# Two eight-batch attention blocks around a latent-attention block: reciprocal norms broadcast inside SBUF, and a new task order in the feed-forward phases

## The chip, the core and the metric

The kernel runs on one core of a Trainium2 chip. A core has five engines with an instruction queue each: TensorE (PE, matrix products), VectorE (DVE), ScalarE (ACT), GpSimd (POOL) and SyncE (SP). In this kernel SP computes nothing: it issues every DMA. Engines wait for one another through semaphores, and each works through its own list strictly in order. The metric is the time on the device in microseconds, the median of several executions.

## The reference

The input x is [8, 512, 128] in fp32. It passes through three residual blocks:

```python
x = x + 0.5 * ffn(layernorm(x), ...)      # phase 1, two layers
x = x + attn(layernorm(x), ...)           # the latent-attention block
x = x + 0.5 * ffn(layernorm(x), ...)      # phase 3, the same two layers again
```

What is called ffn holds two layers, and each layer is a local attention followed by a gated feed-forward part:

```python
h = shift_token(x)                         # half of the channels come from the token before
q, k, v = split(h @ wqkv)                  # 8 heads of 64
q = l2norm(q) * qs;  k = l2norm(k) * ksc   # l2norm(t) = t / ||t||, per token and head
q, k = rotary_xpos(q, k)
o = local_attention(q, k, v)               # windows of 64, own window and the one before, softmax
x = x + o @ wo
h = layernorm(shift_token(x)) * lg + lb
a, g = split(h @ w1 + b1)                  # HID = 341
x = x + (a * gelu(g)) @ w2 + b2
```

The part that the change touches is l2norm: a sum of squares over the 64 channels of each head, the power -1/2 of it, and a multiplication of q and k with it.

## The kernel before

**The layout.** Channels or heads lie on partitions, the 512 tokens of a batch element (T) on the free axis. A feed-forward phase (`ffn_phase`, run twice) handles 16 units: unit u is layer u // 8 of batch element u % 8. A unit passes through some thirty tasks. Each engine has a loop over n and runs in each iteration a list of tasks for the units n+1, n, n-1, ..., n-4, so up to five units are in flight (a software pipeline). The list, `run(task, n - k, ...)`, is a table written out by hand for each engine; that order and the semaphores decide everything, and no scheduler is at work. One iteration in the steady state is called a cycle below, and it advances every unit by one place. Eight PSUM banks are handed from task to task with `claim`, which makes PE wait until the last reader of a bank is done.

**q and k.** `project(u, m)` for m = 0..3 multiplies with wqkv in a split precision (three matmuls for each half) into banks 4 and 5. (m even: q, m odd: k; the pair 0, 1 serves heads 0 to 3, the pair 2, 3 heads 4 to 7.) ACT squares the two banks into `SQ[:, m, 0]` and `SQ[:, m, 1]` (`square_a`, `square_b`). DVE multiplies each bank with the rotary tables into `TP` (`rotate(u, m, 1)` and `rotate(u, m, 0)`, L782), and POOL combines these into `QK[:, m]` (`rotate`, L936 and L937). There is one `TP`: DVE may fill it for m+1 only after POOL has read it for m (`ad_ok`).

**The norms.** After the fourth square PE sums them over the heads (`norms`, L467; below "the norm sums") into a bank in which partition 8j holds one of sixteen rows (m, i): pair m, head i of the group. DVE clamps (`clamp`, L788), ACT forms exp(-0.5 ln) (L657, L658), and DVE makes one Newton step (`norms`, L793 to L796). Now RN holds 16 reciprocal norms, in rows of 512 tokens. They have to stand on all 32 partitions of their head before POOL can multiply `QK` with them. SP does this with a trip through DRAM: it stores `RN[0:P:8]` to `norms_d` (L363), waits for it to land (`r_out`), waits until POOL no longer needs the old values (`nr_ok`), and loads them back with four broadcasting DMAs, each into 32 partitions of `SQ[:, :, 1]` (L369). POOL waits for all four (`r_in`) and multiplies `QK[:, m]` with `SQ[:, m, 1]` (`norms`, L942). The first group of scores needs m = 0 and 1, the second m = 2 and 3.

**Attention.** `scores(u, g)` (L475 the mask, L484 the products) fills banks 0 to 3 for heads 4g to 4g+3. DVE takes the maxima (L805), PE transposes them (`turn_max`), DVE spreads them (`spread_max`, L812 and L816), PE adds them to the scores (`add_max`, L498), ACT exponentiates (`softmax_exp`). PE sums (`sums`, L506), ACT inverts the sums, SP sends them through DRAM (`sums_d`, L380 and L386) into `OT`. PE multiplies with v (`attend`, L517), DVE multiplies by the inverse sums (`attended`, L823), and PE applies wo (`join`, L527).

**The gated part.** `center`, `variance`, `hidden` (six thirds, L552), `gate`, `gated` (L848) and `outward` (L560) follow, with the variances sent through DRAM as well (`vars_d`, L391). `statistics` and `tokens` on DVE, `tokens` (L435) on PE bring in the next batch element (layer 0 only); `back` takes it out. `values` (L456) makes v, `high` and `low` (L633, L928) split the next unit's input into two parts, on which the next `project` waits.

**The queue of SP** runs in each iteration values, variances, sums for group 0, sums for group 1, norms.

**The latent-attention block** (`mla_phase`) lies between the two phases and takes its folded weights `Wq_s`, `Wk_s`, `Wv_s` from tiles that the setup wrote and that stay in SBUF during phase 1.

## Time and profile before

| | us |
|---|---|
| median of 3 runs | 2268.1 (2256.44 to 2269.57) |
| the profiled execution, its time | 2281.34 |
| the profiled execution, its span | 2279.2 |

| busy share of the span | PE | PE weight loads | DVE | ACT | POOL |
|---|---|---|---|---|---|
| whole kernel | 81% | 49% | 63% | 49% | 40% |

The setup ends at about 43 us, the first feed-forward phase at 917 us, the latent-attention block between 918 and about 1440 us, and the second feed-forward phase fills the rest. The granted clock of TensorE is 0.915 in the mean.

How to read it: a row of the timeline gives the start, the duration, the engine, the line and the operation, `x4` for four that follow one another, and in square brackets the idle time of the engine ahead of it with what ended it. `SPq` is the issue of a DMA by SP. A matmul of 512 fp32 columns counts as two instructions there. A row of the waits gives the engine that waited, for whom, the sum in us, how many times, and the longest. A row of the windows gives for a stretch the busy time of each engine, PE's granted clock (1.00 is 2.4 GHz, 0.50 is 1.2 GHz), the busy share of the DMA engines and the GB/s that they moved.

### The profile page before, as it was taken

To read this page: it belongs to the slowest core of one execution; us is meant where nothing else is said; L and a number is where in the kernel's file an instruction comes from. 1 tells how busy PE (TensorE), PEld (TensorE's weight loads), DVE (VectorE), ACT (ScalarE), POOL (GpSimd) and SP (SyncE) were. 2 spreads that over 40 slices of the span, in tenths; PEclk is the share of its full clock that TensorE was granted. 3 is DMA by queue.
4 is the path that set the end of the run, shared out by engine and by line. 5 is a ranking of instruction groups with operands and counts; after the bars stand their busy time and mean duration, and the time that the engine had idled before them with its cause. 6 is when DMAs were issued, how large, how long until landed. Compare 5 with 4: busy or idle time off the path is not lost. (4 is left out here: it accounts for less than half of the span.)

```text
span 2279.2 us, 50236 instructions
## 1 busy us (share of the span) xinstructions
PE 1837.4 (81%) x20010; PEld 1120.2 (49%) x20074; DVE 1444.4 (63%) x2281; ACT 1117.9 (49%) x2070; POOL 901.3 (40%) x624
## 2 busy tenths in 40 slices
PE   1577888888888787799999996677788888887886
PEld 1344454544555454466666663344454544544543
DVE  2466766566665644688888885566666665555563
ACT  1134444354444433488888884234434444444342
POOL 2444444454444440222222222444544444444440
PEclk9888999899999989799999997789989898999899
DMA  3122223222222321000000000123322222233221
GB/s 123 36 59 61 69 70 93 62 60 66 68 68 73 84 60 29 1 2 1 2 1 2 1 1 1 46 60 87 76 60 60 61 73 60 70 90 77 64 65 42
DMA packets 60664, 118.84 MB, mean 52 GB/s; under 512 B 7519, under 2 KB 17939, under 8 KB 58259
## 3 DMA queue, kind: packets, MB, share of 16 engines
q1 hardware_dynamic: 60435, 115.64, 20.0%
q8 instruction: 162, 2.65, 0.5%
q14 instruction: 67, 0.55, 0.1%
HBM read 82.51 MB, written 3.74 MB: 38 GB/s over the span
## 5 line engine op out<-in xcount | busy, mean ns | idle before, releaser
L942 POOL TENSOR_TENSOR QK<-QK,SQ 128x1024 f32<-128x1024 f32 x128 | 298.3, 2352 | 190.6 <-DMA SQ<-norms_d 190.6
L782 DVE SCALAR_TENSOR_TENSOR TP<-bank,cols,tab 128x1024 f32<-128x1024 f32 x256 | 320.4, 1275 | 47.2 <-PE bank L447 34.5
L805 DVE TRANSPOSE_TENSOR_REDUCE MX<-bank 128x16 f32<-128x512 f32 x256 | 160.4, 684 | 264.6 <-PE bank L484 264.6
L936 POOL TENSOR_TENSOR QK<-TP 128x512 f32<-128x512 f32 x128 | 164.3, 1283 | 407.8 <-DVE TP L782 260.4
L1195 ACT ACTIVATE PL<-bank,NM 128x384 f32<-128x384 f32 (+3 forms) x512 | 255.5, 540 | 15.6 <-DVE NM L1275 12.7
L1275 DVE TENSOR_REDUCE NM<-bank 128x1 f32<-128x384 f32 (+3 forms) x352 | 217.7, 635 | 35.4 <-PE bank L1109 31.7
L475 PE MATMUL bank<-bandb,identb 128*128 128x512 bf16 x192 | 74.5, 510 | 180.8 <-POOL QK L942 178.0
L1118 PE MATMUL bank<-cst,PL 128*128 128x128 f32 x1280 | 200.0, 275 | 3.3 <-DVE PTL L1284 1.1
L639 ACT ACTIVATE SQ<-bank 128x512 f32<-128x512 f32 x128 | 76.5, 598 | 239.7 <-PE bank L447 239.7
L1104 PE MATMUL bank<-KL,QZL 128*128 128x384 f32 (+3 forms) x512 | 189.3, 422 | 2.3 <-DVE QZL L1232 2.3
L484 PEld LDWEIGHTS bank<-QK 32*64 32x64 f32 x8192 | 155.8, 162 | 40.8 <-issue 40.8
L484 PE MATMUL bank<-QK 32*64 32x128 f32 x8192 | 170.1, 322 | 0.3 <-issue 0.3
L1187 ACT ACTIVATE PTL<-bank 128x512 f32<-128x512 f32 (+1 forms) x288 | 161.5, 561 | 13.0 <-PE bank L1118 9.8
L517 PEld LDWEIGHTS bank<-PT,V 128*64 128x64 f32 x4096 | 132.6, 142 | 68.4 <-issue 49.1
L937 POOL TENSOR_TENSOR QK<-TP 128x512 f32<-128x512 f32 x128 | 165.6, 1294 | 0.0
L447 PE MATMUL bank<-HTH,wqkv_h 128*128 128x512 f32 x256 | 136.9, 535 | 25.2 <-DVE TP L782 17.6
L645 ACT ACTIVATE SQ<-bank 128x512 f32<-128x512 f32 x128 | 76.5, 597 | 160.0 <-DVE TP L782 96.3
L1315 POOL TENSOR_SCALAR QZL<-QS,cst 128x512 fp32r<-128x512 f32 x64 | 108.2, 1701 | 116.3 <-DVE QS L1222 116.2
L682 ACT ACTIVATE DC<-bank 128x512 f32<-128x512 f32 x32 | 19.2, 599 | 267.8 <-PE bank L534 267.8
L651 ACT ACTIVATE V<-bank 128x512 f32<-128x512 f32 x128 | 76.5, 598 | 148.2 <-PE bank L456 141.9
L823 DVE TENSOR_TENSOR OT<-bank,OT 128x512 f32<-128x512 f32 x128 | 82.2, 684 | 104.1 <-DMA OT<-sums_d 104.0
L517 PE MATMUL bank<-PT,V 128*64 128x64 f32 x4096 | 145.8, 229 | 0.9 <-DVE OT L823 0.8
(171 smaller groups left out, 3777.1 us busy)
## 6 DMA issues: line engine op xcount, KB each, us to landing
SQ<-norms_d SPq DMA_DIRECT2D x128, 256.0 KB, 4.9
OT<-sums_d SPq DMA_DIRECT2D x128, 256.0 KB, 3.9
V<-V SPq DMA_DIRECT2D x32, 512.0 KB, 7.7
V<-V SPq DMA_DIRECT2D x32, 384.0 KB, 8.8
RB<-vars_d SPq DMA_DIRECT2D x32, 256.0 KB, 3.2
X<-in_L_attn_x SPq DMA_DIRECT2D x8, 256.0 KB, 4.4
out<-X SPq DMA_DIRECT2D x8, 256.0 KB, 8.5
wqkv_raw<-in_L_ffn_wqkv SPq DMA_DIRECT2D x1, 1536.0 KB
```

Source lines behind the costliest of these rows:

```text
L484: last = nc.tensor.matmul(BK[i][e * W:(e + 1) * W, k0:k0 + n], QK[r, 2 * g + 1, z, k0:k0 + W], QK[r, 2 * g, z, k0:k0 + n], start=False, st ...
L517: last = nc.tensor.matmul(BK[k][e * W:(e + 1) * W, w * W:(w + 1) * W], (V1, V0)[w % 2][:, w // 2, h * DH:(h + 1) * DH], PT[:, j // 2, h % ...
L782: nc.vector.scalar_tensor_tensor(out=TP[:, o:o + 2, :], in0=BK[4 + z][:, :].unsqueeze(1).to_broadcast([P, 2, T]), scalar=q, in1=tab[:, e, ...
L805: last = nc.vector.tensor_reduce(MX[:, i, :], BK[i][:, :].rearrange("p (a b) -> p a b", b=32), AX_X, ALU.max, apply_transpose=True)
L936: nc.gpsimd.tensor_tensor(QK[:, m, 0, :], TP[:, 2, :], TP[:, 1, :], ALU.subtract)
L937: nc.gpsimd.tensor_tensor(QK[:, m, 1, :], TP[:, 0, :], TP[:, 3, :], ALU.add).then_inc(S["ad_ok"], 1)
L942: nc.gpsimd.tensor_tensor(QK[:, m, :, :], QK[:, m, :, :], SQ[:, m, 1, :].unsqueeze(1).to_broadcast([P, 2, T]), ALU.mult).then_inc(S["nr_ok ...
L1104: nc.tensor.matmul(bank[:, h * N:(h + 1) * N], QZL[:, G % 2, h0 + h, i * P:(i + 1) * P].bitcast(F32R), KL[:, G % 2, 0:N].bitcast(F32R), st ...
L1118: last = pe.transpose(BK[B_PT[k % 2]][:, j * P:(j + 1) * P], PL[:, k % PRING, j * P:(j + 1) * P], ident)
L1187: nc.scalar.activation(dst, src, ACT.Copy).then_inc(S["pta_ok"], 1)
L1195: last = nc.scalar.activation(PL[:, m % PRING, h * N:(h + 1) * N], BK[m % SRING][:, h * N:(h + 1) * N], ACT.Exp, bias=NM[:, m % SRING, h:h ...
L1275: nc.vector.tensor_reduce(NM[:, m % SRING, 0:n], BK[m % SRING][:, 0:n * N].rearrange("p (h k) -> p h k", h=n), AX_X, ALU.max, negate=True) ...
```

## The change

Four things are changed.

1. The norms no longer go through DRAM. `norms` on SP issues sixteen DMAs from SBUF to SBUF, each of which reads one row of RN (one partition, 2 KB) 32 times and writes it to 32 partitions of a tensor of its own, `RB` (64 KB each, 1 MB for a unit, as before). They are issued m by m, and each m has its semaphore, so that POOL can multiply m = 0 when four of the sixteen have landed.
2. `SQ[:, m, 1]` is no longer written by DMA. ACT's `square_b` waits for the norm sums of the unit before (`ss_in`), and no more for POOL's multiplication.
3. RB takes 8 KB of each partition. U and `stats` shrink, and the folded weights are stored to DRAM during the setup (`folded_d`) and loaded back at the start of the latent-attention block.
4. The order of the tasks in the loops of all five engines is another.

```diff
                         def norms(u):
                             sp.wait_ge(S["nw_ok"], u + 1)
-                            sp.dma_start(norms_d[u % 2], RN[0:P:8, :]).then_inc(S["r_out"], 16)
-                            sp.wait_ge(S["r_out"], 16 * (u + 1))
                             if u >= 1:
                                 sp.wait_ge(S["nr_ok"], 4 * u)
-                            for i in range(4):
-                                src = norms_d[u % 2].rearrange("(c i) n -> i c n", i=4)[i]
-                                sp.dma_start(SQ[32 * i:32 * i + 32, :, 1, :],
-                                             src.unsqueeze(0).broadcast_to([32, 4, T])).then_inc(S["r_in"], 16)
+                            for m in range(4):
+                                for i in range(4):
+                                    src = RN[32 * m + 8 * i:32 * m + 8 * i + 1, :]
+                                    sp.dma_start(RB[32 * i:32 * i + 32, m, :], src.unsqueeze(1).broadcast_to([1, 32, T])).then_inc(S[f"r_in{m}"], 16)
...
                         def square_b(u, m):
                             act.wait_ge(S["nb_ok"], 4 * u + m + 1)
                             if u >= 1:
-                                act.wait_ge(S["nr_ok"], 4 * (u - 1) + m + 1)
+                                act.wait_ge(S["ss_in"], u)
...
                         def norms(u, m):
                             pool.wait_ge(S["ad_ok"], 4 * u + m + 1)
-                            pool.wait_ge(S["r_in"], 64 * (u + 1))
+                            pool.wait_ge(S[f"r_in{m}"], 64 * (u + 1))
...
+                    sp.wait_ge(copied, 8)
+                    sp.dma_start(folded_d, fold[:, :]).then_inc(kept, 16)
+                    sp.wait_ge(kept, 16)
...
                     def _(sp):
+                        sp.dma_start(fold[:, :], folded_d).then_inc(S["fold_in"], 16)
                         for last_use in used:
                             sp.sem_clear(last_use)
...
                         xt(0)
+                        pe.wait_ge(S["fold_in"], 16)
                         values(0)
```

The order on **SP** in the steady state, from one unit's inverse sums to the next variances. Before, with the trip through DRAM:

```order
L380 DMA sums_d<-DR 4x512
L386 DMA OT<-sums_d 64x2x512 x2
L363 DMA norms_d<-RN 16x512
L369 DMA SQ<-norms_d 32x4x512 x4
L374 DMA V_1<-V_1 64x2048
L375 DMA V_1<-V_1 64x1536
L391 DMA vars_d<-RV 4x128
```

And in the changed kernel (its lines are three higher from here on):

```order
L383 DMA sums_d<-DR 4x512
L389 DMA OT<-sums_d 64x2x512 x2
L373 DMA RB<-RN 32x1x512 x16
L377 DMA V_1<-V_1 64x2048
L378 DMA V_1<-V_1 64x1536
L394 DMA vars_d<-RV 4x128
```

The place of the norms in the queue has stayed, behind the second sums and ahead of the copy of v; one store and four loads have become sixteen copies.

On **PE** around the norm sums (`bank<-SQ,cst`). Before, the outward product (`bank<-GL,w_s`) stands behind the norm sums, and one of four attend groups (x16 each) ahead of them:

```order
L498 MATMUL bank<-CB,pick 128x512 x4
L517 MATMUL bank<-PT,V_1 64x64 x16
L467 MATMUL bank<-SQ,cst 32x512 x8
L517 MATMUL bank<-PT,V_1 64x64 x16
L506 MATMUL bank<-PT,ones_0 32x512 x4
L560 MATMUL bank<-GL,w_s 128x512 x3
L517 MATMUL bank<-PT,V_1 64x64 x32
```

Now:

```order
L563 MATMUL bank<-GL,w_s 128x512 x3
L501 MATMUL bank<-CB,pick 128x512 x4
L470 MATMUL bank<-SQ,cst 32x512 x8
L520 MATMUL bank<-PT,V_1 64x64 x16
L509 MATMUL bank<-PT,ones_0 32x512 x4
L438 MATMUL bank<-cst,U 128x128 x4
```

The outward product has moved ahead of the norm sums and an attend group behind them. From there to the next scores the order is hidden, three attend groups, four values, two hidden, join, project 0; before it was two attend groups, four values, two hidden, tokens, join, project 0.

On **DVE** between the maxima of the first score group (`MX<-bank`) and the pair of rotary products (`TP`) of m = 2. Before:

```order
L805 TENSOR_REDUCE MX<-bank 128x16 x4
L782 SCALAR_TENSOR_TENSOR TP<-bank,cols,tab 128x1024
L834 TENSOR_SCALAR VV<-bank 128x128
L812 TENSOR_REDUCE CT<-bank 64x32
L816 TENSOR_TENSOR CB<-CT,place 64x512
L782 SCALAR_TENSOR_TENSOR TP<-bank,cols,tab 128x1024
L848 SCALAR_TENSOR_TENSOR GL<-bank,b_s,GL 114x512
L838 SCALAR_TENSOR_TENSOR VT__1<-RV 128x128
```

Now:

```order
L809 TENSOR_REDUCE MX<-bank 128x16 x4
L838 TENSOR_SCALAR VV<-bank 128x128
L816 TENSOR_REDUCE CT<-bank 64x32
L820 TENSOR_TENSOR CB<-CT,place 64x512
L786 SCALAR_TENSOR_TENSOR TP<-bank,cols,tab 128x1024 x2
L842 SCALAR_TENSOR_TENSOR VT__1<-RV 128x128
```

Both rotary products of m = 1 now stand behind the spreading of the maxima, and PE's project 1 stands behind turn_max.

## Rows read from the trace of the kernel before

**Rows 1.** Windows: busy us of each engine, clock, DMA share, GB/s; second phase.
```profile
1500.00:2200.00 700.00, 576.13 (x7146) 347.75 (x7175) 438.29 (x602) 306.46 (x514) 323.79 (x213) 0.90 0.27 67
```

**Rows 2.** Timeline of SP: store of the norms; first and last of 15 and of 13.
```profile
137.92 0.60 SPq L363 DMA_DIRECT2D norms_d<-RN  x1
...
833.78 0.60 SPq L363 DMA_DIRECT2D norms_d<-RN  x1
...
1586.51 0.60 SPq L363 DMA_DIRECT2D norms_d<-RN  x1
...
2193.66 0.60 SPq L363 DMA_DIRECT2D norms_d<-RN  x1
```

**Rows 3.** Waits from 1540 to 2141 us, which holds 12 cycles.
```profile
PE bank L475 <- POOL QK L942: 69.2, 12, 7.2
POOL QK L942 <- DMA SQ<-norms_d: 62.1, 12, 7.3
```

**Rows 4.** Timeline of PE from one first score group to the next.
```profile
1650.79 1.49 PE L475 MATMUL bank<-bandb,identb 128*128 128x512 bf16 x3 [4.30 <-POOL QK L942]
1652.21 3.69 PE L484 MATMUL bank<-QK 32*64 32x128 f32 x128
...
1665.89 2.03 PE L484 MATMUL bank<-QK 32*64 32x128 f32 x128
...
1677.19 3.50 PE L467 MATMUL bank<-SQ,cst 128*32 128x512 f32 x16
...
1681.71 1.06 PE L506 MATMUL bank<-PT,ones 128*32 128x512 f32 x8
1685.48 2.08 PE L517 MATMUL bank<-PT,V 128*64 128x64 f32 x64
1688.34 0.47 PE L456 MATMUL bank<-wqkv_h,HTH 128*128 128x512 f32 x1 [0.78 <-DVE Z L866]
...
1691.76 0.46 PE L552 MATMUL bank<-HNH,w_h 128*114 128x512 f32 x1
...
1693.66 3.60 PE L527 MATMUL bank<-OT,wo_s 128*128 128x512 f32 x8
1696.69 0.79 PE L447 MATMUL bank<-HTH,wqkv_h 128*128 128x512 f32 x1
...
1703.92 1.49 PE L475 MATMUL bank<-bandb,identb 128*128 128x512 bf16 x3 [5.28 <-POOL QK L942]
```

**Rows 5.** Timeline of SP, DVE and POOL in the same cycle.
```profile
1685.84 1.23 SPq L386 DMA_DIRECT2D OT<-sums_d  x2
1687.12 0.61 SPq L363 DMA_DIRECT2D norms_d<-RN  x1
1691.14 1.29 DVE L823 TENSOR_TENSOR OT<-bank,OT 128x512 f32<-128x512 f32 x2 [1.79 <-DMA OT<-sums_d]
1691.23 1.73 SPq L369 DMA_DIRECT2D SQ<-norms_d  x4
1692.91 1.09 POOL L928 TENSOR_TENSOR HTL<-Z,HTH 128x512 fp32r<-128x512 f32 x1 [5.04 <-ACT HTH L633]
1698.81 6.96 POOL L942 TENSOR_TENSOR QK<-QK,SQ 128x1024 f32<-128x1024 f32 x3 [4.80 <-DMA SQ<-norms_d]
```

**Rows 6.** DMA: landing of the norms' store (L363), and a window with SQ<-norms_d in flight.
```profile
DMA to landing us min/median/max: 2.2/3.6/4.5
2200.00:2202.00 2.00, 2.00 (x6) 0.81 (x5) 0.27 (x1) 0.61 (x2) 0.00 (x0) 1.00 1.08 217
```

**Rows 7.** Timeline of DVE: the pair of rotary products of m = 2.
```profile
1666.51 2.46 DVE L782 SCALAR_TENSOR_TENSOR TP<-bank,cols,tab 128x1024 f32<-128x1024 f32 x2
```

**Rows 8.** Timeline: last fold and last work of the setup; the block's first use of it.
```profile
30.79 0.69 DVE L270 TENSOR_SCALAR Wk_s<-bank 128x512 f32<-128x512 f32 x1
...
39.56 3.06 POOL L199 TENSOR_TENSOR w_l<-w_s,w_h 128x1364 fp32r<-128x1364 f32 x1 [2.51 <-ACT w_h L210]
...
926.68 2.04 PE L1064 MATMUL bank<-Wv_s,XT 128*128 128x128 f32 x8 [0.88 <-DVE XT L1215]
```

More of the change, by code:

```diff
@@ L579, in _ @@
                         for n in range(-3, NU + 4):
-                            run(hidden, n - 3, 1, 0, 5)
-                            run(hidden, n - 3, 1, 1, 7)
-                            run(back, n - 4, 4)
-                            run(tokens, n + 1, 4)
-                            run(join, n - 2, 6)
+                            run(project, n - 1, 1)
+                            run(add_max, n - 2, 0)
+                            run(hidden, n - 4, 0, 1, 7)
+                            run(hidden, n - 4, 0, 2, 6)
@@ new lines, in _ @@
+                            run(project, n - 1, 2)
+                            run(scores, n - 2, 1)
+                            run(sums, n - 2, 0, 6)
+                            run(project, n - 1, 3)
+                            run(turn_max, n - 2, 1, 6)
+                            run(outward, n - 4, 7)
+                            run(add_max, n - 2, 1)
+                            run(norms, n - 1, 6)
+                            run(attend, n - 2, 0, 5)
+                            run(sums, n - 2, 1, 4)
@@ new lines, in _ @@
+                            run(back, n - 4, 7)
+                            run(tokens, n, 7)
+                            run(hidden, n - 3, 1, 0, 6)
+                            run(attend, n - 2, 1, 5)
+                            run(attend, n - 2, 2, 4)
+                            run(attend, n - 2, 3, 5)
+                            run(values, n - 1, 0, 6)
+                            run(values, n - 1, 1, 7)
+                            run(values, n - 1, 2, 6)
+                            run(values, n - 1, 3, 7)
@@ L585, in _ @@
+                            run(hidden, n - 3, 1, 1, 6)
+                            run(hidden, n - 3, 0, 0, 4)
+                            run(join, n - 2, 7)
                             run(project, n, 0)
                             run(scores, n - 1, 0)
[L587 to L591 removed]
@@ L612, in _ @@
-                            run(values, n, 3, 7)
+                            run(center, n - 2, 6)
+                            run(hidden, n - 3, 1, 2, 7)
+                            run(variance, n - 2, 6)
+                            run(turn_max, n - 1, 0, 7)
                     @block.scalar
```

173 lines of the change are left out of this document (78 added, 95 removed).

## Prediction

> **What bounds the kernel now.** I first read the windows. In the second feed-forward phase PE is busy 576 of 700 us and no other engine over 438 [rows 1]: PE leads, but a sixth of its time is idle. Then the length of a cycle. SP stores the norms once per unit, and the stores lie 695.9 us apart over 14 cycles in phase 1 (49.7 each) and 607.2 us over 12 in phase 3 (50.6 each) [rows 2]; the mean is 50.1 us. Two phases of 16 units have 30 such steps, some 1,500 of the 2,279 us. Then the waits: in 12 cycles PE stood before the mask matmul of the first scores for 69.2 us, 5.8 each, for POOL's multiplication, and POOL stood 62.1 us, 5.2 each, for the DMA that brings the norms [rows 3]. So one loop closes the cycle: norm sums on PE, clamp, root, Newton step, DRAM and back, two multiplications on POOL, first scores on PE, and then PE's own list until the next norm sums.
>
> I take one cycle apart, from the norm sums at 1677.19. They end at 1680.69 [rows 4], which I call time 0. SP issues the store at 1687.12, +6.4, since it is busy with the second softmax sums until then; the loads go out at 1691.23, +10.5; POOL starts to multiply at 1698.81, +18.1, and PE starts the scores at 1703.92, +23.2 [rows 4, 5]. From the scores at 1650.79 to 1680.69 it had been 29.9 us [rows 4]. This cycle has 53.1 us, one of the longer ones.
>
> **Stretch A, norm sums to first scores.** The trip's first hop goes: 4.1 us from store to loads [rows 5]. What is left is PE's own work. Between the two ends PE now has four attend groups (two take 2.08, so 4.16), the sums 1.06, then four values, two hidden and tokens, which took 1688.34 to 1693.66, 5.3, and one more hidden (0.8, half of what the two and tokens took between 1691.76 and 1693.66, rounded down for tokens), join 3.0 (start to start) and project 2.0 (estimate: six matmuls, where the three of a value take 0.86, a quarter of 1688.34 to 1691.76, and a start-up) [rows 4]. The sum is 16.3. One wait is in it: a hidden third now uses the bank of the third attend group, which DVE frees after the loaded inverse sums have landed, at 1691.14 or +10.5, plus 0.65 for one of the two products [rows 5]. PE gets there at about +10.5 as well and loses 0.7. **A is 17.0 instead of 23.2.**
>
> That holds if the norms come in time. POOL must first do HTL, which starts 1.15 us after the last value [rows 4, 5] and takes 1.09; with the values ending at about +9.8 POOL is free at +11.8 to +12. Each multiplication takes 2.32 [rows 5]. To be ready at +17.0 the first needs its norms by +12.3 and the second by +14.7, which is 5.9 and 8.3 us after the first issue at +6.4. The trace shows no copy of this kind. From below: issue at the present 0.43 us (1.73 for four) and transfer at the present 217 GB/s [rows 5, 6], 0.3 us per copy, so that issue sets the pace; the eighth issue is over 3.5 us after the first, and the shortest landing of a DMA that reads RN is 2.2 us [rows 6]: 5.7 us, in time by 2.6. From above: each copy is through only when its predecessor is, 2.2 us apiece; the eighth lands after 17.6. The rate of 217 GB/s is nearest to the first, the single source partition speaks for the second. I take the lower end and price the upper one as a rival.
>
> The copy of v and the variances stand behind the norms in SP's queue. Sixteen issues take 16 x 0.43 = 6.9 us, where the store, its landing and four loads take 5.8 now, from 1687.12 to 1692.96 [rows 5]: 1 us later. The copied v is first read a whole cycle on, so this costs nothing; without that cover it would be that 1 us. The inverse sums' loads stand ahead of the copies. The dropped wait of square_b costs and gives nothing while PE's sums are earlier than POOL's product.
>
> **Stretch B, first scores to norm sums.** Behind a wait of 4.3 us the first group of scores took 3.69 us, and the second, with the same products and work ahead of it, 2.03 [rows 4]; the mean granted clock of the phase is 0.90 [rows 1], so part of it is at the lower of the two levels, and I read the difference as that. Without that wait the mask and the scores should take 2.8 instead of 5.1: 2.3 less. The rest, 24.8 us, is a chain of DVE and POOL through the one TP tile: a rotary pair takes DVE 2.46 [rows 7] and then POOL as long, and three pairs follow each other, with maxima and spreads between. The new order makes it longer: project 1 starts after turn_max, for which I choose 0.5, and the statistics (ten small instructions, layer 0 only) now stand in this chain and not behind it, for which I choose 0.7 in the mean; no row prices either alone. PE also has the outward product in this stretch and one attend group and one hidden third less, in time that it waits anyway. I take 24.8 + 1.2 = 26.0. **B is 28.8 instead of 29.9.**
>
> **The sum.** 17.0 + 28.8 = 45.8 us a cycle. Against the mean of 50.1 (not against this long cycle, of which part is chance) 4.3 are saved, over 30 steps 129. The first unit of a phase, which nothing overlaps, saves the 4.1 hop too: 8 for both phases. The setup is free: the fold is ready at 31.5, the store of 0.6 MB takes at 217 GB/s 2.7 us, with the landing of the RN store 4.5 at most about 7, and the setup ends with POOL at 42.6 [rows 6, 8]. Without that cover it would be 7 us. The load is issued at 918 and wanted at 926.7 [rows 8], also later than 7 us. The latent-attention block does not change. Total -137 on the profiled 2281.3, so 2144; the median lies 13 below that execution, which gives 2131, and I say 2135.
>
> A rule speaks against this. The Trainium skill, "SBUF — State Buffer", section "Door 1: The DMA port swizzle", says that a DMA's rate goes with how many of 16 SBUF ports its partitions reach, about 27 GB/s for each. By it the present loads, 32 partitions or 8 ports, get 218 GB/s, and the trace agrees with 217 [rows 6]. By it also a copy that reads a single partition gets 27 GB/s and takes 2.4 us, sixteen of them 38 us if they don't overlap; the page measured a load, and no run here shows a read from one partition. Its result would be a cycle of over 60 us.
>
> **The rivals.**
> (a) *The copies queue on their source: slower, 2420.* Place: the sixteen DMAs, each with one source partition for 16 engines. With 1.9 us apiece the eighth lands at 6.4 + 15.2 = 21.6, the second product ends at 24.0, 7.0 late; the last lands at 36.8, its product ends at 39.2, and the second scores, due at 24.0 + 12.8 = 36.8, are 2.4 late. (They are due 12.8 after the first ones: 13.7 now, from 1652.21 to 1665.89 [rows 4], of which about 1 is left out for the clock.) The cycle is 45.8 + 9.4 = 55.2, and 30 x 5.1 = 153 are added to 2268. At 2.2 apiece the same sum gives 24.0, 26.4 (9.4 late), 44.0 against 39.2 (4.8 late), a cycle of 60.0 and 2565. It decides at 1.6 apiece: 4.6 late, nothing for the last, a cycle of 50.4. Against it: 16 rows from 16 partitions needed no more than 2.2 [rows 6], and sources of different heads can overlap. Chance 0.34.
> (b) *Nothing much, within 1%: 2270.* Copies at 1.5 to 1.7 apiece, or a wait for DVE that eats the gain. POOL would then still wait for a DMA in each cycle for 5 us. Chance 0.12.
> (c) *The chain of DVE and POOL takes half of the gain: 2215.* Statistics, two gated products and the outward sums lie ahead of rotary products; with B at 31.6 the cycle is 48.6, 30 x 1.5 + 8 = 53. For it: DVE is already busy 438 of 700 us [rows 1]. Chance 0.16.
> (d) *PE alone bounds: 2077.* PE is busy 41 us of 50 [rows 1], part of it at half clock. With a cycle of 44.0 it is 30 x 6.1 + 8 = 191. Against it: B hangs on TP. Chance 0.10.
> The forecast, 2100 to 2180, has 0.28.
>
> **How the numbers follow.** Faster by over 1% (what a measurement of this kernel can tell from no change) are the forecast, (c) and (d): 0.54. Within 1% is (b), 0.12; slower is (a), 0.34. The range takes in (d) and reaches to (a)'s own time, 2075 to 2420; below it I leave 0.08 and above it, where the copies take 2 us and more, 0.10. For the faster cases alone it is 2075 to 2220.
>
> **What would show it.** Right: the spacing of the copies' first issues falls to about 46; POOL's wait for a DMA ahead of the multiplication goes from 5.2 to under 1 us a cycle; PE's wait before the first mask goes from 5.8 to under 1; the first score group takes 2.0 instead of 3.7; the copies of one m land less than 4 us after their first issue, and the landings of the four m are about 1.8 apart. Wrong: these landings are 5 us and more apart, the DMA share of the phase is far over the present 0.27 [rows 1] for the same bytes, and POOL waits longer than now; then (a) holds. If POOL does not wait and the cycle is still over 48, the wait has moved to DVE's products or to PE waiting for the banks of project, and (c) holds. A gap at the start of the latent-attention block would show the reloaded weights on the path.

## The result, and the profile after

The changed kernel takes 2169.68 us, the median of 3 runs (2169.38 to 2170.55), against 2268.1 before: a ratio of 0.958, 95% interval 0.953 to 0.963. It is faster by 4.2%. The profiled execution took 2170.55 us, its span is 2168.7.

PE is busy 82% of the span, where it was 81%. From the page of the changed kernel: the DMA queue (packets, MB, share of 16 engines) and the copies (KB, us from issue to landing).

```profile
q1 hardware_dynamic: 65843, 115.79, 31.8%
RB<-RN SPq DMA_DIRECT2D x512, 64.0 KB, 4.0
```

Windows of the changed kernel (columns as in [rows 1]): most of the second phase, 2 us in which the copies are in flight, and 2 us with the copy of v.

```profile
1450.00:2100.00 650.00, 550.43 (x7179) 328.24 (x7178) 462.70 (x618) 302.42 (x511) 327.79 (x213) 0.98 0.45 75
1858.00:1860.00 2.00, 2.00 (x7) 0.95 (x6) 0.75 (x1) 0.00 (x0) 0.01 (x1) 1.00 0.87 81
1868.00:1870.00 2.00, 2.00 (x29) 0.97 (x18) 1.58 (x3) 0.59 (x2) 2.00 (x2) 1.00 1.00 247
```

The granted clock rose from 0.90 [rows 1] to 0.98, and PE is busy 85% of this stretch instead of 82%. The DMA engines are busy 0.45 of it instead of 0.27, for as many bytes in a unit. The two short windows show why: with the copies in flight the engines are busy 0.87 of the time and move 81 GB/s, with the copy of v 247.

Timeline of SP in the changed kernel: the sixteen copies of five units, three of the first phase and two of the second.

```profile
133.17 12.90 SPq L373 DMA_DIRECT2D RB<-RN  x16
...
375.23 11.94 SPq L373 DMA_DIRECT2D RB<-RN  x16
...
780.15 12.38 SPq L373 DMA_DIRECT2D RB<-RN  x16
...
1528.70 12.22 SPq L373 DMA_DIRECT2D RB<-RN  x16
...
2080.92 12.49 SPq L373 DMA_DIRECT2D RB<-RN  x16
```

From 133.17 to 780.15 are 14 cycles, 46.2 us each (49.7 in [rows 2]); from 1528.70 to 2080.92 are 12, 46.0 each (50.6). The mean is 46.1. But the cycles are not alike: the first five take 48.4 (133.17 to 375.23), the other nine 45.0 (375.23 to 780.15). In the first five the next batch element of layer 0 is brought in, by statistics and tokens; they are called layer-0 cycles below, the others layer-1 cycles. Before, the two kinds did not differ (by the stores of the first phase, 49.7 in both).

Waits of the changed kernel from 1500 to 2050 us, 12 cycles (us, times, longest).

```profile
DVE OT L827 <- DMA OT<-sums_d: 52.6, 12, 5.3
POOL QK L946 <- DMA RB<-RN: 38.5, 36, 2.0
PE bank L478 <- POOL QK L946: 26.5, 12, 2.9
```

PE waits for POOL 2.2 us a cycle, where it was 5.8, and POOL for the DMAs 3.2, where it was 5.2 [rows 3]. POOL now waits three times in a cycle, each time briefly.

Timeline of the changed kernel in one cycle of layer 1.

```profile
1844.65 1.92 PE L470 MATMUL bank<-SQ,cst 128*32 128x512 f32 x16
...
1853.06 12.92 SPq L373 DMA_DIRECT2D RB<-RN  x16
...
1857.52 0.46 PE L555 MATMUL bank<-HNH,w_h 128*114 128x512 f32 x1 [0.46 <-DVE OT L827]
...
1859.99 2.36 POOL L946 TENSOR_TENSOR QK<-QK,RB 128x1024 f32<-128x1024 f32 x1 [2.05 <-DMA RB<-RN]
...
1862.89 0.40 PE L450 MATMUL bank<-HTH,wqkv_l 128*128 128x512 f32 x1
1862.90 2.37 POOL L946 TENSOR_TENSOR QK<-QK,RB 128x1024 f32<-128x1024 f32 x1 [0.55 <-DMA RB<-RN]
1865.32 1.04 PE L478 MATMUL bank<-bandb,identb 128*128 128x512 bf16 x4 [2.04 <-POOL QK L946]
1866.29 2.03 PE L487 MATMUL bank<-QK 32*64 32x128 f32 x128
1866.67 2.36 POOL L946 TENSOR_TENSOR QK<-QK,RB 128x1024 f32<-128x1024 f32 x1 [1.40 <-DMA RB<-RN]
...
1889.71 1.92 PE L470 MATMUL bank<-SQ,cst 128*32 128x512 f32 x16
```

The norm sums end at 1846.57, time 0. The copies start at +6.5 and are issued 0.81 us apart. The first four have landed at +13.4, when POOL starts, the next four at +16.3, the third four at +20.1. PE has finished its own list at +16.7 (its last matmul starts at 1862.89) and stands until the scores at +18.75: stretch A is 18.75 us. The next norm sums end at 1891.63: stretch B is 26.3.

The same in a cycle of layer 0.

```profile
1565.73 1.92 PE L470 MATMUL bank<-SQ,cst 128*32 128x512 f32 x16
...
1567.07 1.28 POOL L941 TENSOR_TENSOR QK<-TP 128x512 f32<-128x512 f32 x1
1567.21 2.96 DVE L306 TENSOR_SCALAR U<-X,mv,rstd 128x128 f32<-128x128 f32 x4
1568.30 1.28 POOL L957 TENSOR_TENSOR HNL<-DC,HNH 128x512 fp32r<-128x512 f32 x1
1570.21 0.69 DVE L792 TENSOR_SCALAR VN<-bank 128x512 f32<-128x512 f32 x1
...
1576.45 12.94 SPq L373 DMA_DIRECT2D RB<-RN  x16
...
1588.73 1.04 PE L478 MATMUL bank<-bandb,identb 128*128 128x512 bf16 x4 [2.11 <-POOL QK L946]
...
1613.73 1.92 PE L470 MATMUL bank<-SQ,cst 128*32 128x512 f32 x16
```

Here DVE computes the tokens of the next batch element (L306) ahead of the clamp (L792); it starts them 0.4 us before the norm sums end. The clamp starts 2.6 us after the end of the norm sums, 0.1 after it in the other cycle (1846.64 in the trace, right behind 1846.57), and the copies start at +8.8. A is 21.1, B 26.9.

Taken in this way from the timeline of PE for the steady cycles of the second phase (12 before, 12 after), the means are as below. The first three cycles of each phase of the changed kernel are left out: in them the pipeline is still filling, the tokens are done sooner (the clamp starts 0.1 to 1.4 us after the norm sums), A is 16.7 to 19.0 and B 26.9 to 31.9.

| us | A | B | cycle |
|---|---|---|---|
| before | 22.9 (22.2 to 24.4) | 27.6 (25.6 to 29.9) | 50.5 |
| after, last four layer-0 cycles | 21.3 (20.8 to 21.9) | 27.0 (25.9 to 28.4) | 48.3 |
| after, eight layer-1 cycles | 18.8 (18.4 to 19.4) | 26.4 (25.9 to 27.5) | 45.2 |

### The profile page after: what moved, and what is told of

Read it like the earlier page. It is cut to its first block and busy times, and to the rows that moved or that the text cites. A ratio compares the mean times of both kernels' runs of the same rounds, so it can differ in the third digit from the quotient of the medians.

```text
span 2168.7 us, 50695 instructions
## 1 busy us (share of the span) xinstructions
PE 1785.8 (82%) x20074; PEld 1079.9 (50%) x20074; DVE 1488.3 (69%) x2281; ACT 1112.0 (51%) x2070; POOL 905.7 (42%) x624
## 2 busy tenths in 40 slices
DMA packets 66076, 119.03 MB, mean 55 GB/s; under 512 B 13183, under 2 KB 23603, under 8 KB 63667
## 3 DMA queue, kind: packets, MB, share of 16 engines
q1 hardware_dynamic: 65843, 115.79, 31.8%
## 5 line engine op out<-in xcount | busy, mean ns | idle before, releaser
L946 POOL TENSOR_TENSOR QK<-QK,RB 128x1024 f32<-128x1024 f32 x128 | 302.4, 2363 | 118.6 <-DMA RB<-RN 118.6
L450 PE MATMUL bank<-HTH,wqkv_h 128*128 128x512 f32 x256 | 124.3, 486 | 54.8 <-DVE TP L786 43.6
L932 POOL TENSOR_TENSOR HTL<-Z,HTH 128x512 fp32r<-128x512 f32 x32 | 37.9, 1184 | 304.4 <-ACT HTH L636 304.4
L941 POOL TENSOR_TENSOR QK<-TP 128x512 f32<-128x512 f32 x128 | 164.4, 1284 | 0.0
L487 PEld LDWEIGHTS bank<-QK 32*64 32x64 f32 x8192 | 133.9, 143 | 30.0 <-issue 30.0
L520 PE MATMUL bank<-PT,V 128*64 128x64 f32 x4096 | 140.1, 224 | 10.4 <-DVE OT L827 10.2
L487 PE MATMUL bank<-QK 32*64 32x128 f32 x8192 | 146.7, 291 | 0.0
L670 ACT ACTIVATE PT<-bank 128x512 f32<-128x512 f32 x256 | 132.1, 606 | 27.7 <-PE bank L501 27.7
L1128 PEld LDWEIGHTS bank<-cst,PL 128*128 128x128 f32 x1280 | 139.1, 141 | 8.9 <-issue 5.1
```

The source lines that it names most:

```text
L487: last = nc.tensor.matmul(BK[i][e * W:(e + 1) * W, k0:k0 + n], QK[r, 2 * g + 1, z, k0:k0 + W], QK[r, 2 * g, z, k0:k0 + n], start=False, st ...
L520: last = nc.tensor.matmul(BK[k][e * W:(e + 1) * W, w * W:(w + 1) * W], (V1, V0)[w % 2][:, w // 2, h * DH:(h + 1) * DH], PT[:, j // 2, h % ...
L941: nc.gpsimd.tensor_tensor(QK[:, m, 1, :], TP[:, 0, :], TP[:, 3, :], ALU.add).then_inc(S["ad_ok"], 1)
L946: nc.gpsimd.tensor_tensor(QK[:, m, :, :], QK[:, m, :, :], RB[:, m, :].unsqueeze(1).to_broadcast([P, 2, T]), ALU.mult).then_inc(S["nr_ok"], 1)
L1128: last = pe.transpose(BK[B_PT[k % 2]][:, j * P:(j + 1) * P], PL[:, k % PRING, j * P:(j + 1) * P], ident)
```

## The experiments

All times are medians, the ratio is to the kernel before, on the same chip, with its 95% interval. The kernels ran on several chips, on which the kernel before took between 2257 and 2268 us; a difference in us between two rows can be off by some 10 us for that reason, and where it matters the ratios decide.

| kernel | order of tasks | how the norms travel | us | ratio |
|---|---|---|---|---|
| changed kernel | new | 16 copies from one partition each | 2169.7 | 0.958 (0.953 to 0.963) |
| order_only | new | DRAM, 4 loads, one wait | 2338.6 | 1.036 (1.031 to 1.040) |
| copies_only | old | 16 copies from one partition each | 2123.4 | 0.940 (0.936 to 0.944) |
| one_wait | new | 16 copies, POOL waits for all | 2500.4 | 1.102 (1.096 to 1.107) |
| dram16 | new | DRAM, 16 loads, wait by m | 2161.5 | 0.958 (0.953 to 0.962) |
| dram16_old_order | old | DRAM, 16 loads, wait by m | 2108.7 | 0.929 (0.925 to 0.934) |
| src8 | new | 16 copies from 8 partitions each | 2112.1 | 0.934 (0.930 to 0.939) |
| src8_old_order | old | 16 copies from 8 partitions each | 2073.8 | 0.914 (0.910 to 0.918) |
| no_transfer | new | not at all | 2095.3 | 0.925 (0.921 to 0.929) |
| src8_stats_early | new, one task moved | 16 copies from 8 partitions each | 2095.5 | 0.926 (0.921 to 0.930) |
| four_old_order | old | 4 copies over 128 partitions | 2078.8 | 0.918 (0.914 to 0.922) |
| four_stats_early | new, one task moved | 4 copies over 128 partitions | 2076.4 | 0.917 (0.913 to 0.921) |
| sums_inside | old | 4 copies, inverse sums inside SBUF too | 2061.0 | 0.911 (0.910 to 0.912) |

### The two halves of the change alone

order_only keeps the new order, RB and the setup, and sends the norms through DRAM as before:

```diff
+                            sp.dma_start(norms_d[u % 2], RN[0:P:8, :]).then_inc(S["r_out"], 16)
+                            sp.wait_ge(S["r_out"], 16 * (u + 1))
...
-                            for m in range(4):
-                                for i in range(4):
-                                    src = RN[32 * m + 8 * i:32 * m + 8 * i + 1, :]
-                                    sp.dma_start(RB[32 * i:32 * i + 32, m, :], src.unsqueeze(1).broadcast_to([1, 32, T])).then_inc(S[f"r_in{m}"], 16)
+                            for i in range(4):
+                                src = norms_d[u % 2].rearrange("(c i) n -> i c n", i=4)[i]
+                                sp.dma_start(RB[32 * i:32 * i + 32, :, :],
+                                             src.unsqueeze(0).broadcast_to([32, 4, T])).then_inc(S["r_in0"], 16)
...
-                            pool.wait_ge(S[f"r_in{m}"], 64 * (u + 1))
+                            pool.wait_ge(S["r_in0"], 64 * (u + 1))
```

> The order of the changed kernel, but the norms again go through DRAM: one store of RN, a wait for its landing, four loads into RB, and POOL waits for all four. If the gain comes from the copies, the loads go out 4 us later (about 10.5 us after the norm sums) and land together near 17, the second product ends near 21.7 in place of 18.2 and every cycle is about 3 us longer than in the changed kernel: 2169.7 + 30 x 3 = 2260, with PE waiting about 5 us a cycle for POOL. If the new order alone makes the gain (loads hidden), it stays within 1% of 2170 and PE waits 2 us.

copies_only has the copies, and the task lists of the kernel before on all engines.

> The sixteen copies, RB and the reloaded weights, but the five task lists of the kernel before. If the copies carry the gain, PE reaches the first scores 18.0 us after the norm sums and finds the second product done at about 18.2, so that the old wait of 5.8 us is nearly gone: 2268 - 30 x 4.5 = 2133 to 2170. If the order carries it, PE still waits about 5 us for POOL and the time is within 1% of 2268.

order_only took 2338.6 us, 3.5% over the kernel before. Its timeline (norm sums, store, loads, POOL, scores), and behind it the variances' stores of three units of the second phase:

```profile
1561.69 3.64 PE L473 MATMUL bank<-SQ,cst 128*32 128x512 f32 x16
...
1572.31 0.60 SPq L369 DMA_DIRECT2D norms_d<-RN  x1
1575.82 1.74 SPq L375 DMA_DIRECT2D RB<-norms_d  x4
...
1583.65 6.95 POOL L948 TENSOR_TENSOR QK<-QK,RB 128x1024 f32<-128x1024 f32 x3 [6.08 <-DMA RB<-norms_d]
1588.35 1.89 PE L481 MATMUL bank<-bandb,identb 128*128 128x512 bf16 x4 [6.04 <-POOL QK L948]
...
1550.92 0.54 SPq L397 DMA_DIRECT2D vars_d<-RV  x1
...
1819.79 0.53 SPq L397 DMA_DIRECT2D vars_d<-RV  x1
...
2225.53 0.53 SPq L397 DMA_DIRECT2D vars_d<-RV  x1
```

From the end of the norm sums (1565.33) to the scores are 23.0 us, where the mean before was 22.9: the order takes nothing off stretch A while the trip through DRAM is there. Five layer-0 cycles take 53.8 each (1550.92 to 1819.79), eight of layer 1 50.7 (1819.79 to 2225.53). In this phase the layer-1 cycles are as all were before (50.6 in [rows 2]), the layer-0 cycles 3.1 us longer. Over both phases the profiled spans differ by 56 us, and by SP's stores of the norms 51 of them lie in the first six steps of the two phases, those in which the next batch element is brought in. The expected 2260 was wrong.

copies_only took 2123.4, 46 us less than the changed kernel. The same stores of its variances:

```profile
1479.35 0.54 SPq L394 DMA_DIRECT2D vars_d<-RV  x1
...
2057.36 0.54 SPq L394 DMA_DIRECT2D vars_d<-RV  x1
```

Thirteen cycles of both layers take 44.5 each. So the whole gain comes with the DMAs, and the new order costs in both surroundings: some 46 us with the copies (ratios 0.940 and 0.958) and 81 with the DRAM trip (2338.6 against 2257.3 for the kernel before on the same chip). With the copies, the profiled spans of the two orders differ by 52 us. By the first issues of the copies, the first six steps of each phase are 3.6 us longer each in the new order, 43 together, and the nine others 0.7 each, 13 together: the layer-0 cycles carry most of it.

copies_only also has RB of its own and ACT's `square_b` without its wait for POOL. That dropped wait was not tried alone. In the trace of the kernel before ACT stood 63.5 us for it in 25 waits, but PE's norm sums stood only 4.2 us for these squares, so its share is likely small.

### Is it the missing trip, or the waiting pair by pair?

one_wait is the changed kernel with POOL waiting for all sixteen copies ahead of its first multiplication; dram16 is the new order with the trip through DRAM kept, but sixteen loads with the semaphores of the copies:

```diff
-                            pool.wait_ge(S[f"r_in{m}"], 64 * (u + 1))
+                            for k in range(4):
+                                pool.wait_ge(S[f"r_in{k}"], 64 * (u + 1))
```

> As the changed kernel, but POOL waits for all sixteen copies before its first product, as it waited for all four loads before. The last copy is issued 12.3 us after the first, which goes out 6.5 us after the norm sums, and lands 4 us later, near +23; the second product ends near +28 in place of +18.7 and each cycle is about 9 us longer: 2170 + 30 x 9 = 2440, slower than the kernel before. If landing pair by pair is not what the change lives on (only the hop saved), it stays within 3% of 2170. Same outputs.

```diff
+                            sp.dma_start(norms_d[u % 2], RN[0:P:8, :]).then_inc(S["r_out"], 16)
+                            sp.wait_ge(S["r_out"], 16 * (u + 1))
...
-                                    src = RN[32 * m + 8 * i:32 * m + 8 * i + 1, :]
-                                    sp.dma_start(RB[32 * i:32 * i + 32, m, :], src.unsqueeze(1).broadcast_to([1, 32, T])).then_inc(S[f"r_in{m}"], 16)
+                                    src = norms_d[u % 2][4 * m + i:4 * m + i + 1, :]
+                                    sp.dma_start(RB[32 * i:32 * i + 32, m, :], src.broadcast_to([32, T])).then_inc(S[f"r_in{m}"], 16)
```

> As the changed kernel, but RN is stored to DRAM once and the sixteen broadcasts read their row from there: the same number of DMAs and bytes into the same places, only the source differs. If one source partition at a time slows the copies, the sixteen issues fall from 12.9 us to 7 to 9 us, the DMA share of the phase falls from 0.46 to below 0.35 and the fourfold groups land about 2 us apart; the store's hop then costs 4 us at the start, the second product ends 1 to 2 us later than now and the time is about 2200. If the number of DMAs is what costs, issue stays at 12.9 us for sixteen, the second product is 4 us later and the time is about 2290.

one_wait took 2500.4, 331 us more than the changed kernel and 10% more than the kernel before. Its timeline:

```profile
1606.94 12.65 SPq L373 DMA_DIRECT2D RB<-RN  x16
...
1623.34 6.94 POOL L947 TENSOR_TENSOR QK<-QK,RB 128x1024 f32<-128x1024 f32 x3 [11.55 <-DMA RB<-RN]
1628.43 1.49 PE L478 MATMUL bank<-bandb,identb 128*128 128x512 bf16 x3 [11.68 <-POOL QK L947]
```

The last copy lands 16.4 us after the first issue, and PE stands 11.7 us. In this order the copies are a loss without the semaphore for each m.

dram16 took 2161.5, as long as the changed kernel (both ratios are 0.958); neither of its two expected values (2200, 2290) was right, both too high. Its timeline of SP and POOL, and then its page's row on the loads:

```profile
1620.58 0.61 SPq L369 DMA_DIRECT2D norms_d<-RN  x1
1625.30 7.27 SPq L376 DMA_DIRECT2D RB<-norms_d  x16
...
1628.69 7.00 POOL L948 TENSOR_TENSOR QK<-QK,RB 128x1024 f32<-128x1024 f32 x3 [2.98 <-DMA RB<-norms_d]
```

```profile
RB<-norms_d SPq DMA_DIRECT2D x512, 64.0 KB, 2.0
```

The hop costs 4.7 us in this cycle, but the sixteen loads are issued in 7.3 instead of 12.9 and land in 2.0 us instead of 4.0, and POOL starts 8.1 us after the store, where in the changed kernel it starts 6.9 after the first copy. What the copies win by leaving DRAM out they give back in issue and landing. In the old order it is the same, and clearer:

> The lists of the kernel before and the trip through DRAM with one store, but sixteen loads with a semaphore for each m in place of four loads with one. In the new order this form was as fast as the copies inside SBUF (2161 against 2170). If landing m by m is the whole gain, it takes about as long as the copies in the old order: 2115 to 2130. If the saved hop is worth something here, it is slower by 1 to 3 us a cycle: 2150 to 2215.

2108.7, where the copies in the same order took 2123.4 (ratios 0.929 and 0.940). Leaving DRAM out is not what made the kernel faster.

### What holds the copies up

src8 lets each copy read all eight partitions that hold its row (the norm sums' matrix writes each of the sixteen rows on eight partitions):

```diff
-                                    src = RN[32 * m + 8 * i:32 * m + 8 * i + 1, :]
-                                    sp.dma_start(RB[32 * i:32 * i + 32, m, :], src.unsqueeze(1).broadcast_to([1, 32, T])).then_inc(S[f"r_in{m}"], 16)
+                                    src = RN[32 * m + 8 * i:32 * m + 8 * i + 8, :]
+                                    sp.dma_start(RB[32 * i:32 * i + 32, m, :], src.unsqueeze(1).broadcast_to([8, 4, T])).then_inc(S[f"r_in{m}"], 16)
```

> As the changed kernel, but each copy reads the eight partitions that hold the same row (four destinations from each) in place of one partition 32 times. If the source partition is the limit, eight partitions are two groups of four with a path each and the transfer of sixteen copies falls from 13 us to about 7, the DMA share from 0.46 to about 0.33, PE's wait from 2.0 to below 1 us a cycle: 2169.7 - 30 x 1.5 = 2125. If issue or the number of DMAs is the limit, nothing changes: 2170.

2112.1, 58 us less (ratios 0.958 and 0.934), with the same bytes, number of DMAs and order. Its page's row on the queue, then PE's wait in the same stretch as above, then its timeline with POOL's first two multiplications of a unit:

```profile
q1 hardware_dynamic: 61747, 115.77, 23.0%
```

```profile
PE bank L478 <- POOL QK L946: 9.5, 12, 2.1
```

```profile
1638.61 11.54 SPq L373 DMA_DIRECT2D RB<-RN  x16
1644.07 2.35 POOL L946 TENSOR_TENSOR QK<-QK,RB 128x1024 f32<-128x1024 f32 x1 [0.42 <-DMA RB<-RN]
1646.91 2.39 POOL L946 TENSOR_TENSOR QK<-QK,RB 128x1024 f32<-128x1024 f32 x1 [0.49 <-DMA RB<-RN]
```

The share of the DMA engines' time fell from 31.8% to 23.0%, PE's wait from 2.2 to 0.8 us a cycle, and the norms of m = 0 and 1 are there 5.5 and 8.3 us after the first issue instead of 6.9 and 9.8. SP's issue has changed less: 0.72 us apiece instead of 0.81. The edit also changes into how many packets a copy is cut: its page counts 9,087 packets under 512 B where the changed kernel has 13,183, eight fewer for each of the 512 copies. That this is not what helps is seen from dram16. It writes to the same places with sixteen DMAs and has 13,695 such packets, but reads its rows from DRAM, and its queue's share is 20.6%. So it is reading from a single partition that slows the copies.

src8_old_order is src8 with the task lists of the kernel before.

> The lists of the kernel before with the sixteen copies, each reading eight source partitions. With one source partition this order took 2123 and PE still waited 1.8 us a cycle for POOL's product; if eight source partitions take most of that wait away as they did in the new order (2.0 to 0.8), 2123 - 30 x 1.2 = 2087. If the old order then waits for something else right behind, such as the join for the inverse sums, it stays at 2115 to 2125.

2073.8 (ratio 0.914): the source costs some 50 us in the old order too (0.940 before), and the new order some 40 with the faster source (0.934).

no_transfer sends no norms at all; POOL multiplies with a constant, so the kernel computes something else:

```diff
-                            for m in range(4):
-                                for i in range(4):
-                                    src = RN[32 * m + 8 * i:32 * m + 8 * i + 1, :]
-                                    sp.dma_start(RB[32 * i:32 * i + 32, m, :], src.unsqueeze(1).broadcast_to([1, 32, T])).then_inc(S[f"r_in{m}"], 16)
...
-                            pool.wait_ge(S[f"r_in{m}"], 64 * (u + 1))
```

> As the changed kernel, without the sixteen copies: RB is set to a constant once and the norms are never sent, so the output is not the reference's and POOL waits for no DMA. It prices what is left of the norms' trip in the new order. If the copies still cost PE its 2.0 us a cycle and nothing else is behind them, 2170 - 30 x 2 = 2110, the same as with eight source partitions (2112). If they also delay the other transfers on SP and the DMA engines (inverse sums, v, variances), clearly below 2100.

2095.3. In the new order the copies as they are cost some 75 us, and with eight source partitions some 20. With the transfer gone altogether, the new order is still slower than the old one with a transfer (2073.8).

### Why layer 0 is longer

src8_stats_early moves the statistics, ten small instructions on DVE, out of the chain of rotary products, to a later place in DVE's list:

```diff
                             run(maxima, n - 2, 1)
-                            run(statistics, n)
                             run(rotate, n - 1, 3, 1)
...
+                            run(statistics, n + 1)
                             run(attended, n - 2, 2, 4)
```

> The new order with eight source partitions (2112 us), and statistics on DVE moved from the chain of rotary products to the place where DVE waits for the inverse sums. In the new order the cycles of layer 0 are 3.3 us longer than those of layer 1 (46.5 against 43.2), in the old order they are alike. If statistics in that chain are the reason, layer 0 falls to about 43.5 and the time to 2112 - 14 x 3 = 2070, that of the old order with the same copies (2074). If other work of layer 0 (tokens, arrive) is the reason, or the move delays the products of the inverse sums, it stays above 2100.

2095.5, 17 us less than src8, where 42 were expected. By the stores of the variances the layer-0 cycle went from 46.5 to 45.1, with 43.3 in layer 1: the statistics were 1.4 of the extra. The rest, about 2, matches the tokens, which hold back the clamp by 2.5 us in the rows of layer 0 above, and the 2.5 by which A is longer in layer-0 cycles of the changed kernel; that the tokens are the cause was read from the traces and not tried.

The traces say two things more. First, the late copies are not the only way by which the tokens lengthen A: in no_transfer, where no norms travel and PE does not wait for POOL, A is still 18.6 to 19.5 in the steady layer-0 cycles and 16.3 to 17.1 in layer 1. The products with the inverse sums also stand behind the tokens on DVE, and PE waits for these. Second, the tokens became longer by moving. In the kernel before they stand 7.5 us behind the norm sums, ahead of a wait for the inverse sums [rows 5], and POOL is idle:

```profile
1688.23 1.12 DVE L302 TENSOR_SCALAR U<-X,mv,rstd 128x128 f32<-128x128 f32 x4
```

In the changed kernel the same four instructions take 2.96 us, of which the first two, beside POOL's products (L941 and L957 above), take 1.2 and 1.3 and the others 0.3 each. Over the whole trace of the changed kernel, the 52 instructions of L306 with POOL idle take 0.33 to 0.35 us each, and the 32 with POOL at work for over nine tenths of their time 1.2 to 2.8, 1.3 in the median (the 12 in between, half of their time or less, take no longer than with POOL idle). In the kernel before only 6 of the 96 meet POOL in this way. So some 1.8 of the 2.5 us come from what POOL does at that time.

### Fewer issues, and the second trip

four_old_order replaces the four copies of one m by one, which reads 32 partitions and writes 128:

```diff
-                                for i in range(4):
-                                    src = RN[32 * m + 8 * i:32 * m + 8 * i + 1, :]
-                                    sp.dma_start(RB[32 * i:32 * i + 32, m, :], src.unsqueeze(1).broadcast_to([1, 32, T])).then_inc(S[f"r_in{m}"], 16)
+                                src = RN[32 * m:32 * m + 32, :]
+                                sp.dma_start(RB[:, m, :], src.unsqueeze(1).broadcast_to([32, 4, T])).then_inc(S[f"r_in{m}"], 16)
```

> The lists of the kernel before and one copy inside SBUF for each m in place of four: 32 source partitions (each head's norm stands on eight) to all 128 partitions, 256 KB, with a semaphore for each m. Four issues of 0.6 us in place of sixteen of 0.75, and twice the source and destination partitions at a time. With sixteen copies from eight partitions this order took 2074. If PE still waits there for the second product, it goes: about 2050. If the join or POOL's other work is next behind it, 2065 to 2075.

four_stats_early puts the same four copies into the order of src8_stats_early.

> The new order with statistics moved and one copy for each m. PE's wait for POOL should be gone; what is left is the chain of rotary products. If the new order is then as good as the old one, within 1% of the same copies in the old order; if its tighter place of the norm sums pays once the landing is short, 10 to 40 us faster than that.

2078.8 and 2076.4. The copies were issued in 1.0 us each in the median (0.7 in four_stats_early) and landed in 4.9; in the steady state POOL no longer waited for them. four_old_order is no faster than src8_old_order (the intervals overlap), since the wait that it removes was already small. With four copies and the statistics moved, the two orders are equal.

sums_inside is four_old_order with the inverse softmax sums also copied inside SBUF:

```diff
-                            sp.dma_start(sums_d[n % 2], DR[0:P:32, :]).then_inc(S["d_out"], 16)
-                            sp.wait_ge(S["d_out"], 16 * (n + 1))
...
-                            for e in range(2):
-                                src = sums_d[n % 2].rearrange("(j e) n -> e j n", e=2)[e]
-                                sp.dma_start(OT[W * e:W * e + W, 2 * g:2 * g + 2, :],
-                                             src.unsqueeze(0).broadcast_to([W, 2, T])).then_inc(S[("d0_in", "d1_in")[g]], 16)
+                            for j in range(2):
+                                src = DR[W * j:W * j + W, :]
+                                sp.dma_start(OT[:, 2 * g + j, :],
+                                             src.unsqueeze(1).broadcast_to([W, 2, T])).then_inc(S[("d0_in", "d1_in")[g]], 16)
```

> The kernel with one copy for each m in the old order (2079 us), and the inverse softmax sums also copied inside SBUF: two copies for each group, 64 source partitions (each sum stands on 32) to 128, in place of a store, its landing and two loads. The hop of 1.7 us falls away twice a cycle, and on SP the copies of the norms are issued 1.7 us earlier. DVE now waits 4.2 us a cycle for these sums and the join on PE stands behind it. If that wait is the next bound, 1 us or so a cycle is gained: about 2050. If the chain of rotary products bounds, or if copies inside SBUF land later than loads from DRAM (4.9 against 3.9 us) and give the hop back, it stays within 10 us of 2079.

2061.0, the fastest of all: 5.0% under the changed kernel, 8.9% under the kernel before, and 18 us under four_old_order (ratios 0.911 and 0.918), where about 30 were expected. The copies of the inverse sums landed in 3.5 us (its page), not later than the loads from DRAM (4.0). A row of its waits from 1500 to 2050 us, and the window of the same stretch:

```profile
DVE OT L824 <- DMA OT<-DR: 21.7, 12, 4.2
```

```profile
1500.00:2050.00 550.00, 495.68 (x6344) 295.10 (x6367) 382.37 (x521) 276.64 (x458) 274.99 (x179) 0.98 0.33 79
```

DVE waits 1.8 us a time for the inverse sums, where it was 4.4 in the changed kernel, and PE is busy 90% of the stretch.

## Why the prediction was right, and where its numbers were off

The forecast was 2135 with 0.54 for faster; the time is 2169.7. The mechanism, a cycle closed by the norms' way to POOL, with less of it once the norms of each m land by themselves, is what one_wait, dram16 and src8 show. The steps one by one:

**The bound and the cycle: right.** The cycle fell from 50.1 to 46.1, forecast 45.8. In the middle of the phases that is 4.0 us a step where 4.3 were expected.

**Stretch A, PE's own list: right.** Forecast 16.3 and a wait of 0.7 for DVE; PE was through at +16.7, with a wait of 0.46.

**"I take the lower end": the term that was mis-sized.** The prediction took 0.43 us an issue, and put the eighth landing 5.7 us after the first issue, with 8.3 allowed. Measured were 0.81 an issue and 4.0 from issue to landing, and the eighth was there after 9.8 us (+6.5 to +16.3). The second product so ended 2.0 us late, and A is 18.75 instead of 17.0. This is rival (a)'s mechanism at less than its price: a copy from one partition is slow (81 GB/s at 0.87 busy engines, and 58 us of the time by src8), but copies with different sources overlap. With 0.81 apiece they stayed below the 1.6 from which (a) would have decided. The upper bound, each copy through only when its predecessor is, did not occur. The Trainium skill, "SBUF — State Buffer", section "Door 1: The DMA port swizzle", gives a DMA that reaches one port about 27 GB/s, by which 64 KB take 2.4 us, an estimate. The landing of 4.0 and the gain of src8 agree with its direction. Sixteen copies that don't overlap (38 us) are excluded by one_wait, where the last has landed 16.4 us after the first issue.

**Stretch B: the change of it right, its size not.** Forecast 28.8 instead of 29.9, 1.1 less; in the means it went from 27.6 to 26.6 (12 cycles of both kinds). The first score group fell from 3.69 to 2.03, as said. But the 29.9 of the cycle that was taken apart were four cycles' in twelve, the longest there are. The prediction saw that this cycle was long and measured its 45.8 against the mean of 50.1, as if chance had lengthened A and B alike. It was B nearly alone (A 23.2 against a mean of 22.9, B 29.9 against 27.6). So B came out 2 us too high and A 1.8 (layer 1) to 4.3 (layer 0) too low, and the two cancel: that 45.8 lies within 0.3 of 46.1 is in part luck.

**The new order: the step that was missed.** The statistics were put at 0.7 us in the mean, 1.4 in a layer-0 cycle, and that is what src8_stats_early gave. The tokens ahead of the clamp, in stretch A, were not seen at all, though DVE's new list has them there; the copies start at +8.8 instead of +6.5, and A is 2.5 longer. The cycle that it took apart was itself one of layer 0, with 1.1 us of tokens on DVE, but at a place where DVE waited anyway; at the new place they are ahead of the clamp and take 3.0. The prediction costed the order at 1.2 us a cycle and let PE's list in A shrink through it; copies_only shows that the same A (18.4 to 19.6 in its cycles) is had with the old order, and that the new one costs some 46 us.

**The sum.** Of the 137 us that were forecast on the profiled execution, 110.5 came (2279.2 to 2168.7). The 26 steps that [rows 2] cover gave 104 (48.9 and 54.9), forecast 112; the four steps at the starts of the phases, which the prediction had counted like the others, gave nothing (by the first issues of SP they are 4 longer together), forecast 17; the starts and ends of the phases gave 11, forecast 8. The rest of the 35 us between 2135 and 2169.7 is in the last line: the prediction took off the 13 us by which the profiled execution of before lay over its median, while that of after lies only 1 over its own, and it rounded up by 4.

**The edits without a cost: right.** Rows of the changed kernel: store of the folds, last work of the setup; load and first use.

```profile
31.18 0.37 SPq L186 DMA_DIRECT2D folded_d<-fold  x1
...
39.23 3.06 POOL L203 TENSOR_TENSOR w_l<-w_s,w_h 128x1364 fp32r<-128x1364 f32 x1 [2.51 <-ACT w_h L214]
...
863.31 0.33 SPq L1048 DMA_DIRECT2D fold<-folded_d  x1
...
871.77 2.04 PE L1073 MATMUL bank<-fold,XT 128*128 128x128 f32 x8 [0.88 <-DVE XT L1225]
```

The setup ends as before with POOL at 42.3, and the first use still waits for DVE and not for the load.

**The signs.** The spacing and the first score group came as named. POOL's wait was to be under 1 us a cycle and is 3.2, PE's under 1 and is 2.2, the norms of one m were to be there within 4 us and 1.8 apart, and are 6.9 and 2.9 to 3.8. One of the signs named for (a) came too, the DMA share of 0.45 instead of 0.27 for the same bytes; the other two, landings 5 us apart and a longer wait of POOL, did not. These were the signs that the copies are slower than assumed, and they point at the right term.

## What to carry to other kernels

Give each piece of a transfer its own semaphore, in the order in which it is used, before asking which way the bytes should go: in the same order the route moved the time by 3% at most, and the single wait for sixteen copies by 15%. When a row is broadcast from SBUF, read it from all partitions that hold a copy; one DMA over 128 destination partitions was as fast as four over 32, with a quarter of the issues. Look at what POOL does beside DVE at the place to which a task is moved. Time a new order of tasks apart from the edit that it comes with, and take several cycles of each kind apart before one of them stands for all.

## What the runs showed of the hardware that was not expected

A copy of 64 KB from one SBUF partition to 32 lands 4.0 us after its issue in the median, the same broadcast from DRAM 2.0 us, and in the second phase SP issues sixteen of the one in 12.0 to 13.3 us and of the other in 7.3 to 8.5. With eight source partitions the first four have landed after 5.5 us instead of 6.9, and the sixteen are issued in 11.5 to 12.1. Why SP takes longer to issue a DMA whose source is SBUF was not settled. A DMA that reads 32 partitions, each four times, and writes 128 (256 KB) is issued in about 1.0 us and lands in 4.9.

An instruction of DVE that subtracts and multiplies 128 columns from SBUF to SBUF took 0.34 us with POOL idle and 1.2 to 2.8 us with POOL at work on tensors in SBUF for over nine tenths of that time.
